# A metaformer layer on one core: the second norm without its mean, the mean carried as a 97th row, variances in four column groups

## The reference

```python
t = _ln_c(x)                       # norm over the 96 channels of each pixel
# windows of 16 x 16 pixels, 14 apart, 19 x 19 of them in each image:
y = _layernorm(tok, norm1_w, norm1_b)
q, k, v = y @ wq, y @ wk, y @ wv   # 4 heads
tok = softmax(q k^T / 4) v @ wproj + tok
x2 = windows added up, overlaps averaged
y = _gelu(_layernorm(tok2, norm2_w, norm2_b) @ fc1_w + fc1_b)
y = y + _gelu(depthwise_5x5(y) + dw_b)
x = x + (y @ fc2_w + fc2_b + tok2)
x = x + ffn(_ln_t(x))              # in rounded fp8 and fp16 formats
```

## Time and profile before

| | us |
|---|---|
| median of 3 runs | 10127.56 |
| the profiled execution | 10134.36 |
| its span | 10132.5 |
| PE busy in the span | 8854.8 (87%) |
| DVE busy | 5580.2 (55%) |
| ACT busy | 4596.0 (45%) |

### The profile page before, as it was taken

One profiled execution on the slowest core, in us unless ns is written; L12 is line 12 of the kernel. 1 busy time (PEld: TensorE's weight loads), 2 busy tenths in 40 slices (PEclk: granted clock), 3 DMA queues, 4 the chain that ended last, 5 costly groups with the idle time before them and its releaser, 6 DMA issues.

```text
span 10132.5 us, 200877 instructions
## 1 busy us (share of the span) xinstructions
PE 8854.8 (87%) x73708; PEld 5392.1 (53%) x73708; DVE 5580.2 (55%) x10186; ACT 4596.0 (45%) x8600; POOL 1891.9 (19%) x1660
## 2 busy tenths in 40 slices
PE   7776999999999999996898989898989898989898
PEld 3333444444444444443566666666666666666665
DVE  5655777777777777774434343434443444443444
ACT  2222555555555555553344444444444444444443
POOL 0000333333333333332010101010101010101010
PEclk8887999999999999997999999999999999999999
DMA  4433333333333333335111111111111111111110
GB/s 113 121 114 95 86 86 86 89 85 88 94 79 94 86 86 86 89 94 58 29 30 36 30 36 30 36 30 36 30 36 30 36 30 36 30 36 30 36 30 21
DMA packets 473959, 609.18 MB, mean 60 GB/s; under 512 B 169864, under 2 KB 409066, under 8 KB 448650
## 3 DMA queue, kind: packets, MB, share of 16 engines
q1 hardware_dynamic: 473496, 602.66, 24.5%
HBM read 394.17 MB, written 165.49 MB: 55 GB/s over the span
## 4 chain that ended last, share of the span: by engine, by line
PE 34%; DVE 8%; ACT 6%; issue 4%; SPq 1%; DVEq 0%; ACTq 0%; DMA 0%; POOLq 0%; POOL 0%
PE P L1248 6%; PE P L1239 5%; PE P L1115 5%; PE P L1165 4%; ACT H L1313 4%; PE P L1090 3%; PE P L1095 3%; DVE H L1471 2%; PE P L1128 2%; PE P L1123 2%; DVE H L1464 2%; DVE Z L1486 2%; PE P L1268 1%; ACT L1301 1%; ACT L1323 1%
## 5 line engine op out<-in xcount | busy, mean ns | idle before, releaser
L796 DVE TENSOR_REDUCE NM<-P 128x2 f32<-128x512 f32 x2888 | 1910.5, 688 | 743.6 <-PE P L633 734.6
L748 ACT ACTIVATE PROB<-P 128x512 f32<-128x512 f32 x2888 | 1491.3, 603 | 1213.7 <-PE P L648 1213.7
L1165 PE MATMUL P<-FC,XN 97*126 97x192 f32 x5408 | 1121.3, 356 | 140.3 <-ACT Y L1323 139.4
L1064 POOL TENSOR_TENSOR T<-T,Y 96x512 f16 (+1 forms) x260 | 299.0, 1150 | 4679.4 <-DVE Y L1475 4679.4
L1165 PEld LDWEIGHTS P<-FC,XN 97*126 97x126 f32 x5408 | 1019.2, 209 | 265.8 <-ACT Y L1323 176.4
L633 PE MATMUL P<-KB,QB 32*128 32x256 bf16 x5776 | 868.1, 281 | 195.5 <-DVE QF L790 106.9
L648 PE MATMUL P<-QF,KS 32*128 32x256 f32 x11552 | 958.0, 414 | 0.0
L1435 DVE TENSOR_TENSOR X<-X,P 96x512 f32<-96x512 f32 x364 | 248.8, 683 | 1188.4 <-PE P L1090 1188.4
L1307 ACT ACTIVATE SQ<-Z 96x512 f32<-96x512 f32 x260 | 163.7, 630 | 1497.2 <-DVE Z L1451 1282.8
L633 PEld LDWEIGHTS P<-KB,QB 32*128 32x128 bf16 x5776 | 249.4, 94 | 1075.5 <-DVE QF L790 528.0
L656 PE MATMUL P<-PROB,V 128*32 128x256 f32 x11552 | 803.1, 397 | 1.5 <-ACT PROB L748 1.5
(11 more groups left out here) (133 smaller groups left out, 13387.8 us busy)
## 6 DMA issues: line engine op xcount, KB each, us to landing
RBC<-sums SPq DMA_DIRECT2D x456, 160.0 KB, 3.1
X<-x2map SPq DMA_DIRECT2D x52, 1344.0 KB, 8.4
XHS<-xhat SPq DMA_DIRECT2D x76, 768.0 KB, 8.4
RNS<-rnorm SPq DMA_DIRECT2D x38, 1536.0 KB, 9.4
x2map<-XHS SPq DMA_DIRECT2D x76, 768.0 KB, 5.2
T<-in_x SPq DMA_DIRECT2D x52, 960.0 KB, 11.1
out<-T SPq DMA_DIRECT2D x52, 960.0 KB, 4.9
X<-in_x SPq DMA_DIRECT2D x32, 1536.0 KB, 13.2
```

The costliest lines, as they stand in the source:

```text
L748: A.activation(PROB[:, par, u, :], P[:, B_ST[u], :], ACT.Exp, scale=DQ ** -0.5).then_inc(act_exp, 1)
L796: V_.tensor_reduce(NM[:, :, 32 * u + DQ], P[:, B_S[u], :].rearrange("p (a m) -> p a m", a=2), axis=AX.X, op=ALU.max).then_inc(dve_max, 1)
L1165: m = M.matmul(P[0:KW, 5 + (r + 2) % 3, i * MLP:(i + 1) * MLP], xnf[:, RI * WX * w:RI * WX * w + KW], FC1[:, :], start=True, stop=True)
```

## The change

What it does: the projection weights `WP` get a 97th column, the mean of each row over the 96 outputs, and that mean is subtracted from the 96 columns. So the projected values sum to nothing over the channels (as the normed map nearly does), and the 97th output is the mean that was taken away. `XH`, `xhat` and `x2map` get a 97th row (partition) for it, zero in `xhat` at first. The residual addition runs on 97 partitions. The map stage loads rows 0 to 95 of `x2map` into X2, and row 96 of the strip apart (1 x 2560) into a 97th row of `T`; POOL copies it to a 97th row of `Z` (`means`), and a row of ones in `FC2` adds it back in fc2. `mean2`, `centre2` and their waits are gone; the squares are taken from X2 as loaded.

The variances of both norms are summed in four column groups of PE: four matmuls of 128 columns, each writing 32 partitions of one bank, in place of two of 256 columns writing 96. DVE copies the bank to `VS` (`sum2`, `sum3`) and one matmul with `REP` (`gather2`, `gather3`) adds the groups up and lays them out for the three parts. The root, the reciprocal and its parts work on 128 columns in place of 256. The spreads are four matmuls of 128 columns in place of two of 256.

```diff
-        XH = sb("XHS", [C, 2, PATCH, W])
+        XH = sb("XHS", [C + 1, 2, PATCH, W])
-        WP = sb("WP", [128, C])
+        WP = sb("WP", [128, C + 1])
...
+            sp.dma_start(xhat[C, :, :].rearrange("b n -> (b n)").rearrange("(p e) -> p e", p=128),
+                         ACCO[:, 0:B * H * W // 128 // PATCH, :].rearrange("c x r -> c (x r)")).then_inc(z_stored, 16)
+            sp.wait_ge(z_stored, 16)
...
-            zrow = ACCO[0:C, 0:B * 2 * W // PATCH, :].rearrange("c x r -> c (x r)").rearrange("c (b n) -> c b n", b=B)
+            zrow = ACCO[0:C + 1, 0:B * 2 * W // PATCH, :].rearrange("c x r -> c (x r)").rearrange("c (b n) -> c b n", b=B)
...
-                T.matmul(P[0:C, B_CK, :], WP[:, :], af[:, ck(c)], start=True, stop=True).then_inc(pe_out, 1)
+                T.matmul(P[0:C + 1, B_CK, :], WP[:, :], af[:, ck(c)], start=True, stop=True).then_inc(pe_out, 1)
...
-                V_.tensor_tensor(x, P[0:C, B_CK, :].rearrange("c (w r) -> c r w", r=PATCH), x, ALU.add).then_inc(dve_out, 1)
+                V_.tensor_tensor(x, P[0:C + 1, B_CK, :].rearrange("c (w r) -> c r w", r=PATCH), x, ALU.add).then_inc(dve_out, 1)
...
+            def means(u):
+
+                G.tensor_copy(Z[C:C + 1, 0, 0:TO].rearrange("c (x y) -> c x y", y=RO),
+                              TM[C:C + 1, bass.ds(half_of(pool, u), TO)].rearrange("c (y x) -> c x y", x=W)).then_inc(pool_m, 1)
...
             def var2(v, j):
                 pe.wait_ge(act_sq, v * NL + (j + 1))
-                for c in (2 * j, 2 * j + 1):
-                    m = M.matmul(P[0:C, 7, 0:CW], SSEL[:, NCH - 1 - c:NCH - 1 - c + C], SQ[:, 2 + j % 2, (c % 2) * CW:(c % 2 + 1) * CW],
-                                 start=(c == 0), stop=(c == RI - 1))
+                for q in range(4):
+                    c = 4 * j + q
+                    m = M.matmul(P[32 * q:32 * q + 32, 4, 0:CV], SSEL[:, NV - 1 - c:NV - 1 - c + 32], SQ[:, 2 + j % 2, q * CV:(q + 1) * CV],
+                                 start=(j == 0), stop=(j == NL - 1))
                 m.then_inc(pe_var, 1)
+
+            def gather2(v):
+                pe.wait_ge(dve_vs, v + 1)
+                M.matmul(P[0:C, 5, 0:CV], REP[:, :], VS[0][:, :], start=True, stop=True).then_inc(pe_rep, 1)
...
             def first_half(n12, n6, v):
                 for k in range(2 * NZ):
+                    if v is not None and k % 2 == 0:
+                        square2(v, k // 2)
...
-                    if v is not None and q < 4:
-                        for j in range(2 * q, min(2 * q + 2, NL)):
-                            square2(v, j)
-                if v is not None:
-                    std2(v)
+                    if v is not None and q == 0:
+                        std2(v)
...
             def first_half(n7, steps2, v):
...
-                for j in range(NL):
-                    centre2(v, j)
+                sum2(v)
                 dve.wait_ge(act_std, v + 1)
-                parts(STD, RB[0], CW, steps2, dve_parts2, lambda i: back(n7, i - 1))
-                back(n7, 5, 6)
+                parts(STD, RB[0], CV, steps2, dve_parts2)
+                back(n7, *range(NB))
```

More of the change, by code:

```diff
@@ L865, with map_stage @@
 NCG = C // (2 * GP)
[L868 removed]
+def map_stage(nc, x, n2w, n2b, fc1w, fc1b, dww, dwb, fc2w, fc2b, w1, b1, w2, b2, ident, pick, rep, spread, taps, inside,
               x2map, out, nstrip=NS2):
@@ L1104, in spread2, with fc2 @@
                     pe.wait_ge(dve_xn, v * NL + (j - 1))
-                for c in (2 * j, 2 * j + 1):
-                    m = M.matmul(P[0:C, 5 + j % 2, (c % 2) * CW:(c % 2 + 1) * CW], BSEL[:, c, :], RB[0][:, :], start=True, stop=True)
+                for q in range(4):
+                    m = M.matmul(P[0:C, 5 + j % 2, q * CV:(q + 1) * CV], BSEL[:, 4 * j + q, :], RB[0][:, :], start=True, stop=True)
                 m.then_inc(pe_bc, 1)
-            def fc2(nx, j):
+            def fc2(nx, j, n1):
+                if j == 0:
+                    pe.wait_ge(pool_m, n1)
                 if j >= 2:
@@ L1114, in fc2 @@
                 for half in range(2):
-                    m = M.matmul(P[0:C, j % 2, 0:px.stop - px.start], FC2[:, half, :], Z[:, half, px], start=(half == 0), stop=(half == 1))
+                    m = M.matmul(P[0:C, j % 2, 0:px.stop - px.start], FC2[0:C + 1 - half, half, :], Z[0:C + 1 - half, half, px], start=(half == 0), stop=(half == 1))
                 m.then_inc(pe_fc2, 1)
@@ L1126, in var3, with gather3 @@
                 pe.wait_ge(act_sq3, n5 + (j + 1))
-                for c in (2 * j, 2 * j + 1):
-                    m = M.matmul(P[0:C, 4, 0:CW], SSEL[:, NCH - 1 - c:NCH - 1 - c + C], SQ[:, j % 2, (c % 2) * CW:(c % 2 + 1) * CW],
-                                 start=(c == 0), stop=(c == 2 * NF - 1))
+                for q in range(4):
+                    c = 4 * j + q
+                    m = M.matmul(P[32 * q:32 * q + 32, 4, 0:CV], SSEL[:, NV - 1 - c:NV - 1 - c + 32], SQ[:, j % 2, q * CV:(q + 1) * CV],
+                                 start=(j == 0), stop=(j == NF - 1))
                 m.then_inc(pe_var3, 1)
+            def gather3(n1):
+                pe.wait_ge(dve_vs3, n1)
+                M.matmul(P[0:C, 4, CV:2 * CV], REP[:, :], VS[1][:, :], start=True, stop=True).then_inc(pe_rep3, 1)
             def spread3(n5, j):
@@ L1134, in spread3 @@
                     pe.wait_ge(dve_t8, n5 + j)
-                for c in (2 * j, 2 * j + 1):
-                    m = M.matmul(P[0:C, 4, (c % 2) * CW:(c % 2 + 1) * CW], BSEL[:, c, :], RB[1][:, :], start=True, stop=True)
+                for q in range(4):
+                    m = M.matmul(P[0:C, 4, q * CV:(q + 1) * CV], BSEL[:, 4 * j + q, :], RB[1][:, :], start=True, stop=True)
                 m.then_inc(pe_bc3, 1)
@@ L1409, in _, with parts @@
             V.memset(Y1[96:128, :, :], 1.0).then_inc(dve_w, 1)
-            def parts(std, rb, n, v0, done, fill):
+            def parts(std, rb, n, v0, done):
                 steps = [0]
@@ L1417, in small @@
                     ins.then_inc(dve_step, 1)
-                    fill(steps[0])
                     dve.wait_ge(dve_step, v0 + steps[0])
@@ L1526, in second_half @@
                 out16(n5, NF - 1)
-            for j in range(NL):
-                centre2(0, j)
+            sum2(0)
             dve.wait_ge(act_std, 1)
-            parts(STD, RB[0], CW, 1, dve_parts2, lambda i: None)
+            parts(STD, RB[0], CV, 1, dve_parts2)
             for j in range(NL):
@@ L1579, in constants @@
     inside = np.stack([inside[t:t + RI].T.reshape(-1) for t in tops])
-    return ident, stat, bcast, share, qrows, taps, inside
+    pick = np.zeros((C, NV - 1 + 32), f)
+    pick[:, NV - 1] = 1.0 / C
+    rep = np.zeros((128, C), f)
+    spread = np.zeros((C, NV, C), f)
+    for c in range(NV):
+        for k in range(3):
+            spread[32 * k + c, c, :] = 1.0
+            for g in range(4):
+                rep[32 * g + c, 32 * k + c] = 1.0
+    return ident, stat, bcast, share, qrows, pick, rep, spread, taps, inside
 def kernel(**inputs):
@@ L1588 @@
     arrays = {f"in_{n}": np.ascontiguousarray(a) for n, a in inputs.items()}
-    for n, a in zip(("ident", "stat", "bcast", "share", "qrows", "taps", "inside"), constants()):
+    for n, a in zip(("ident", "stat", "bcast", "share", "qrows", "pick", "rep", "spread", "taps", "inside"), constants()):
         arrays[f"const_{n}"] = a
@@ L1604 @@
               conv("fc2_w"), conv("fc2_b"), ffn("W1"), ffn("b1"), ffn("W2"), ffn("b2"),
-              const("ident"), const("stat"), const("bcast"), const("taps"), const("inside"), x2map, out)
+              const("ident"), const("pick"), const("rep"), const("spread"), const("taps"), const("inside"), x2map, out)
     r = run_bass_kernel_spmd(nc, [arrays], core_ids=[0])
```

187 lines of the change are left out of this document (107 added, 80 removed).

## The result

The changed kernel takes 14149.27 us (median of 4 executions, 14143.49 to 14156.69) against 10137.4 us (4 executions, 10114.91 to 10151.69) before: a ratio of 1.3961, 95% interval 1.393 to 1.3991. It is 40% slower, 4012 us. The forecast was 15440, between 12900 and 17000.

A forecast was written before the change was run, and what follows sets the result against it. PE was taken to bound both stages, with DVE's waits for small copies touching its path in the attention stage. 10134 us, plus 6149 for the attention stage, minus 842 for the map stage, gave 15440; range 12900 to 17000.

The forecast's parts named there:

- One engine for 97 rows: Attention stage: each 97-row store or fetch runs on one DMA engine, since 25 rows moved at 5/16 of 96 rows' rate.
- d = 45 us: Attention stage: time of one 97-row transfer of 1552 packets on one engine, between 29 and 51 us.
- 4d - 25: Attention stage: sum of a strip's stalls, with d the time of one 97-row transfer; 155 us a strip.
- The three stalls: DVE's waits per attention strip: A 35 us (RSC copies behind store 1), B 80 (KS copies), C 40 (next group's RSC copies).
- 6 us a strip for the clock: Attention stage: PE comes back from each stall at the lower clock, 2 us for each, 6 a strip.
- The ends: Attention stage outside the 36 full strips: first strip 75 us, last 71, start 125, final wait for two stores 82.
- The map stage, -842: Map stage: 16.5 us less a pass over 51 passes, -842 us in all, between -600 and -1000.
- The transposes, -3: Map stage: all of `parts` moves ahead of the transposes, under the convolution, saving 3 us a pass.
- The transfers stay wide: Rival, attention stage: 97-row transfers stay spread over engines, no stalls, only the map stage counts; 9300 us, chance 0.12.
- Only the engine's load: Rival, attention stage: small copies slip past, only the one engine's load counts; 204 us a strip, 13180 us, chance 0.08.
- SP held: Rival, attention stage: SP waits with the issue, sums go out later, another 40 us a strip; 16900 us, chance 0.08.
- The map stage gives nothing: Rival, map stage: the work taken off PE is not on its path; 16280 us, no chance of its own given.

The follow-up runs named there:

- The stores' experiment: The changed kernel with both stores of a strip issued by ACT on its own queue, except the last strip's: 13621.99 us, ratio 1.3449 to the kernel before.
- the experiment: The changed kernel, transfers split in 96 rows and 1, with the pieces of `parts` put back between DVE's additions: 9386.93 us, ratio 0.9264 to the kernel before.
- six engines: The changed kernel with 102 rows in XHS, xhat and x2map, zeros beyond the 97th: 9809.44 us, ratio 0.9685 to the kernel before.

## Why the prediction was right, point by point

**One engine for 97 rows: right.** The step rested on 5/16. The packets of 25, 97, 102 and 106 rows and the time of 98 bear it out. The section of the Trainium skill on the increment by 16 ("DMA: Bandwidth & Descriptors") that the prediction weighed states what the runs show.

**d = 45 us: mis-sized, and it carries the miss of the total.** An engine alone moves 42.5 packets of 512 bytes a us, 36.5 us for 1552. The prediction took an engine's rate from stretches in which sixteen ran (30.6 a us) or ran out (18.6 GB/s); alone it moves 22. The second reading was closer than it looks: it divided by the share, and where few engines are busy the share counts 1.15 for each. If it did so in the earlier trace rows, the same row gives 18.6 x 1.15 = 21.4 GB/s, and d is about 37. The bounds of 29 and 51 held it. 4d - 25 with 36.5 is 121 in place of 155, 34 us over 36 strips, 1224 of the 1290 us by which the forecast was too high. The rest is made up of smaller misses of both signs: the clock and the ends were put too high by 140 and 46 us, the map stage's gain too high by 45, and the stalls come out 58 us above the formula.

**The three stalls: right in place and order.** With d = 36.5 the steps give A 26.5, B 63 and C 31. Measured, less what DVE waited at the same places before: 29.96, 63.6 and 32.9. Over 36 strips the sum can be checked whole, from the first to the last fetch of rnorm. What DVE waited for in the kernel before (953.4 to 4518.7 us) and in the changed one (1041.6 to 9115.6 us; total us, times, longest):

```profile
DVE NM L796 <- PE P L633: 696.8, 1169, 3.9
DVE QF L790 <- PE P L640: 118.6, 245, 2.3
DVE KB L785 <- DMA KS<-QS: 99.3, 62, 3.7
DVE RSC L804 <- DMA RSC<-OS: 39.8, 49, 1.8
```

```profile
DVE KB L794 <- DMA KS<-QS: 2292.6, 50, 64.7
DVE RSC L813 <- DMA RSC<-OS: 2260.7, 98, 34.6
DVE NM L805 <- PE P L637: 721.6, 1134, 1.8
DVE QF L799 <- PE P L644: 169.0, 273, 2.5
```

The waits for transfers grew from 139.1 to 4553.3 us, 122.6 a strip, where the formula gives 121. The stores' experiment moved A alone away, as a queue kept in order would have it, and showed that B is long because the engine has two transfers, not because the queue has.

**6 us a strip for the clock: right in kind, too large.** Over the stall from 3070 to 3140 us the granted clock is 0.59, and in the stretch right behind it (3142 to 3146) it is 0.50, the lower of the two levels; from 3181 to 3220 us, with PE busy 37.2 of 39 us, it is 0.91. The same work of PE takes 3432.6 us over the 36 strips in place of 3262.1, 4.7 us a strip more. DVE's waits for PE, in the rows above, grew from 815.4 to 890.6 us, 2.1 a strip. That, with 122.6 for the transfers and 0.3 of DVE's own work, makes 125.0 of the 125.3 us. So some 2 us of the slower work reach the time, not 6. That the clock is the whole reason of these 2 us wasn't tested.

**The ends: 353 us forecast, 307 measured.** They hold the same d and were not taken apart. With the strips' 4511 this is the 4818 that stood at 6149.

**The map stage, -842: right, 797 measured.** A pass takes 85.9 us in place of 101.4 (49 passes from the second to the last), -15.5 where -16.5 was forecast, on the first fetch of each, before and after:

```profile
L1012 SPq DMA_DIRECT2D X<-x2map x50: 326/329/340, 4935.9 to 9904.2; - x50
```

```profile
L1028 SPq DMA_DIRECT2D X<-x2map x50: 323/323/339, 9733.4 to 13943.6; - x50
```

The variance's records are 0.045 us apart and not 0.032 (0.36 us for eight), 0.7 us a pass for `var2` and 0.5 for `var3`. That is about the missing us; the other small terms were not measured one by one. The prediction had halved the spacing of records of 256 columns, and at 128 columns the spacing came out above half. If column groups had not overlapped, the upper bound of the step, the map stage would have given 390 less.

The 0.013 us more for each record would also fit a drain at each change between tiling modes, which the prediction priced at 0.063 us. Two packs in a row speak against it:

```profile
11803.31 0.84 PE L1158 MATMUL P<-SQ,SSEL 96*32 96x128 f32 x16
11804.08 0.92 PE L1199 MATMUL P<-FC,XN 97*126 97x192 f32 x4
```

Sixteen records take 0.77 us with the same two changes around them, more than twice the 0.36 of eight, so no part of the 0.36 is fixed. What is left of the gain, some 400 us, is the mean's matmuls and the shorter chain of root and parts, which were not taken apart further.

**The transposes, -3: right in size (3.4), wrong in cause.** The prediction laid it to `parts` moving ahead of `back`. That is 0.5; the rest is left for the early root, which the experiment kept, and no run moved it alone. That the sum came out right here is luck.

**The rivals.** *The transfers stay wide*, 9300: excluded, though it is where the kernel lands once the transfers are split (9347). *Only the engine's load*, 204 us a strip with d = 45 and 170 with d = 36.5: excluded by 224.3. *SP held*: SP is held, for 34 to 38 us an issue, in one strip of the changed kernel:

```profile
3066.19 0.28 SPq L412 DMA_DIRECT2D x2map<-XHS  x1
3066.57 34.47 SPq L423 DMA_DIRECT2D XHS<-xhat  x1
3101.24 38.17 SPq L383 DMA_DIRECT2D KS<-QS  x4
```

But what it delays would have waited on the engine behind the same transfers. DVE's waits for transfers are only 1.6 us a strip above the formula, so it costs about that at most here, not 40. With six engines it is up to 6 of the 12. *The map stage gives nothing*: excluded by 797.

The version to keep has the change and 98 rows: 9323.91 us, a ratio of 0.9192 to the kernel before; with the transfers split in 96 and 1 it is 9347.31, the same within what can be measured.

## What to carry to other kernels

Count the rows of every transfer that a change of shape touches: a 97th row cost 4813 us by itself, a 97th and a 98th together cost nothing. When a transfer comes down to few engines, price it by what is queued behind it on that engine and by who waits for those, since the small copies decide, not the bytes; another queue lets them pass, but the engine is still shared. And judge a change of two effects by its parts: here a gain of 8% was hidden under a loss of 47%, and one more row of zeros brought it back.

## What the runs showed that was not expected

- One engine alone moves 512-byte packets at 42.5 a us (23.5 ns each), two at 42.5 and six at 41.5 each; with sixteen active it is 30.6 each.
- An issue on SP can last almost as long as the long transfer ahead of it: a fetch held SP for 34.5 us behind one store of 1552 packets on one engine (36.5 us), and for 6.2 us behind one of 272 packets on each of six engines (6.6 us).
- Two queues with long transfers on one engine got half of it each (425 and 425 packets in 20 us).
- The share that the transfer view shows counts some 1.15 for each busy engine where few are busy (7.2, 14.3 and 42.6% for one, two and six of 16).
- The granted clock of PE was 0.70 over the 36 strips, in which PE was busy 43% of the time, with stalls of 30 to 65 us. At the two levels, 1.2 and 2.4 GHz, the same work of PE took only 5% longer (3432.6 us in place of 3262.1), since the clock was 0.91 in the stretch of work from 3181 to 3220 us.
